# The output projection leaves PSUM through ScalarE, tile 0 shares a bank with tile 2, and GpSimd computes deviation and centre

## What is computed

```python
xn = layernorm(x)                       # mean and variance of each token, eps 1e-5
q, k, v = split(xn @ Wqkv.T + bqkv)     # 16 heads of 16 channels
q, k = rope(q), rope(k)
att = softmax(mask(q @ k.T / sqrt(16))) # causal, 512 x 512 for each head
s = (att @ v) @ Wo.T + bo
g = silu(xn @ sum(factors) / sqrt(8) + bias)
return x + s * g
```

## Time and profile before

| | us |
|---|---|
| median of 3 runs (237.33 to 238.42) | 238.38 |
| the profiled execution, its own time | 237.23 |
| its span | 235.4 |
| PE busy | 219.1 |
| DVE busy | 170.1 |
| ACT busy | 137.7 |
| POOL busy | 109.1 |

### The profile page before, as it was taken

One profiled execution on the slowest core, in us unless ns is written; L12 is line 12 of the kernel. 1 busy time (PEld: TensorE's weight loads), 2 busy tenths in 40 slices (PEclk: granted clock), 3 DMA queues, 4 the chain that ended last, 5 costly groups with the idle time before them and its releaser, 6 DMA issues.

```text
span 235.4 us, 5723 instructions
## 1 busy us (share of the span) xinstructions
PE 219.1 (93%) x2257; PEld 146.3 (62%) x2257; DVE 170.1 (72%) x262; ACT 137.7 (58%) x268; POOL 109.1 (46%) x91
## 2 busy tenths in 40 slices
PE   6999989889979989999989999999999999899992
PEld 2478857566656555656856566658766565585562
DVE  7677999926799875776988859768975796932223
ACT  2422561457932296698525996785168558868940
POOL 7885397362930080192282800672590007029912
PEclk9999999979985899999999999999999999999999
DMA  6996504201510043034009400026034200002002
GB/s 193 348 357 169 161 25 161 89 3 63 172 37 6 3 144 126 8 105 165 4 7 247 158 3 6 3 87 219 11 111 161 93 10 0 4 6 92 0 3 89
DMA packets 15790, 21.47 MB, mean 91 GB/s; under 512 B 2068, under 2 KB 9236, under 8 KB 15764
## 3 DMA queue, kind: packets, MB, share of 16 engines
q1 hardware_dynamic: 15248, 20.06, 26.4%
q0 software_dynamic: 192, 0.52, 0.9%
q10 hardware_dynamic: 324, 0.52, 0.7%
HBM read 6.16 MB, written 2.10 MB: 35 GB/s over the span
## 4 chain that ended last, share of the span: by engine, by line
PE 74%; DVE 17%; issue 4%; ACT 3%; POOL 0%; DVEq 0%; POOLq 0%
PE ring_ps L484 16%; PE ring_ps L521 10%; DVE rowmax L835 9%; PE ring_ps L550 9%; PE ring_ps L607 8%; PE ring_ps L626 7%; PE ring_ps L502 5%; PE ring_ps L494 5%; PE ring_ps L570 3%; PE ring_ps L617 3%; PE ring_ps L676 2%; PE ring_ps L642 2%; ACT probs L942 2%; PE ring_ps L681 2%; DVE y L855 1%
## 5 line engine op out<-in xcount | busy, mean ns | idle before, releaser
L835 DVE TENSOR_REDUCE rowmax<-ring_ps 128x2 f32<-128x1024 f32 (+3 forms) x86 | 86.7, 1046 | 19.4 <-PE ring_ps L502 18.8
L942 ACT ACTIVATE probs<-ring_ps 128x512 f32<-128x512 f32 x160 | 83.7, 611 | 26.5 <-PE ring_ps L502 19.7
L521 PE MATMUL ring_ps<-stack_k,stack_q 62*128 62x512 f32 (+3 forms) x256 | 42.5, 384 | 4.8 <-DVE rowmax L835 4.1
L502 PE MATMUL ring_ps<-ident_bf,masks 64*128 64x64 bf16 (+1 forms) x704 | 39.8, 210 | 0.0
L550 PE MATMUL ring_ps<-stack_q,stack_k 64*128 64x128 f32 (+3 forms) x256 | 37.4, 361 | 1.8 <-DVE rowmax L835 1.8
L484 PE MATMUL ring_ps<-probs,vaug 128*17 128x256 f32 (+3 forms) x528 | 37.8, 426 | 0.7 <-ACT probs L942 0.7
L521 PEld LDWEIGHTS ring_ps<-stack_k,stack_q 62*128 62x128 f32 x256 | 22.9, 193 | 16.3 <-issue 8.9
L502 PEld LDWEIGHTS ring_ps<-ident_bf,masks 64*128 64x128 bf16 x704 | 20.1, 98 | 12.5 <-issue 6.7
L484 PEld LDWEIGHTS ring_ps<-probs,vaug 128*17 128x17 f32 x528 | 13.8, 97 | 21.5 <-issue 16.5
L709 POOL TENSOR_TENSOR parts<-parts,by_sin 128x512 f32<-128x512 f32 x7 | 9.0, 1281 | 39.4 <-DVE by_sin L812 39.4
L550 PEld LDWEIGHTS ring_ps<-stack_q,stack_k 64*128 64x128 f32 x256 | 21.6, 191 | 8.9 <-issue 5.3
(11 more groups left out here) (94 smaller groups left out, 283.1 us busy)
## 6 DMA issues: line engine op xcount, KB each, us to landing
stack_q<-parts SPq DMA_DIRECT2D x48, 128.0 KB, 2.6
stack_k<-parts SPq DMA_DIRECT2D x42, 128.0 KB, 2.6
probs<-factors SPq DMA_DIRECT2D x2, 1024.0 KB, 8.9
out<-result SPq DMA_DIRECT2D x8, 256.0 KB, 2.5
xbuf<-x SPq DMA_DIRECT2D x3, 512.0 KB, 8.2
xbuf<-x SPq DMA_DIRECT2D x2, 256.0 KB, 2.7
probs<-wqk SPq DMA_DIRECT2D x2, 256.0 KB, 5.1
stack_k<-parts POOLq DMA_DIRECT2D x4, 128.0 KB, 3.6
```

Source lines behind the costliest of these rows:

```text
L502: return pe.matmul(diagonal[:, :, half * ROWS:(half + 1) * ROWS], masks[rows, of_maxima, half, :], own, start=False, stop=(half == 1))
L521: pe.matmul(ps[:, s * width:(s + 1) * width], qk[b % 2][0][rows, h // SIDES, tile * P:(tile + 1) * P], qk[b % 2][1][rows, h // SIDES, 0:wi ...
L835: dve.tensor_reduce(of_both, keys, AX_X, ALU.max).then_inc(taken[kind], 2)
L942: act.activation(probs[:, chunk % PROB_SLOTS, :], ps[:, :], ACT.Exp, scale=float(HD) ** -0.5).then_inc(taken[kind], 1)
```

## The change

The output projection's copy out of PSUM moves from DVE to ACT in batches 0 to 2, as a plain copy. The bias now enters as in batch 3 for every batch: GpSimd multiplies gate by bias and adds it to x in the `gate` step, two more instructions of 128x1024 for batches 0 to 2.

A head's tile 0 product goes to the last 128 columns of the bank that holds its tile 2 product. A group has 10 chunks in 5 pairs. PE issues as many products as before. The four masks of such a pair reach over two blocks of 64 columns each (tile 2's and tile 0's), and the four masks of the tile 0 pair are gone: 64 mask matmuls fewer in all. DVE takes such a pair with two reductions, one for each tile: 7 for a group where there were 6.

Deviation and centre are four GpSimd instructions of 128x4. DVE's two are gone. GpSimd also makes the low part of the output weight. The times of all steps and the list of joined pairs are new (18 maxima pairs and 23 scores pairs where there were 20 and 22).

```diff
-MAX_CHUNKS = 12
+MAX_CHUNKS = 10
...
     if c < 8:
-        return 2, [h + c - 4]
-    return (1 if c < 10 else 0), [h + c % 2, h + 2 + c % 2]
+        return [(2, [h + c - 4], 0), (0, [h + c - 4], 3 * P)]
+    return [(1, [h + c % 2, h + 2 + c % 2], 0)]
...
-             ("gate_tanh", 0, 1.217), ("stack", 2, 1.225), ("gate", 0, 1.304), ("shift", 0, 1.329), ("stack", 3, 1.677),
+     ("gate_tanh", 0, 1.232), ("shift", 0, 1.353), ("gate", 0, 1.431), ("stack", 3, 1.518), ("shift", 1, 1.896),
...
             for half in range(SIDES):
-                for ps, tile, heads in both:
-                    width = (tile + 1) * P
-                    keys = ps[:, 0:count_heads * width].rearrange("p (h k) -> p h k", k=width)
-                    mm = masked(pe, keys[:, :, tile * P:], 1, side(heads[0]), half)
+                for ps, parts_of in both:
+                    tile, heads, col = parts_of[0]
+                    last = (len(heads) * (tile + 1) if len(parts_of) == 1 else QT) - 1
+                    diagonal = ps[:, :].rearrange("p (n k) -> p n k", k=P)[:, tile:last + 1:max(last - tile, 1), :]
+                    mm = masked(pe, diagonal, 1, side(heads[0]), half)
...
-                    after(last)
-                    if b > 0:
-                        dve.wait_ge(s_xn, normalised(b - 1))
-                    dve.tensor_scalar(rstd[:], moments[:, :, 1], EPS, None, ALU.add).then_inc(s_moments, 1)
-                elif kind == "centre":
-                    dve.wait_ge(s_pow, count("rstd", b))
-                    dve.scalar_tensor_tensor(out=centre[:], in0=moments[:, :, 0], scalar=-1.0, in1=rstd[:],
-                                             op0=ALU.mult, op1=ALU.mult).then_inc(s_rstd, 1)
+                    last.then_inc(s_moments, 1)
...
+                elif kind == "project_o" and b < B - 1:
+                    act.wait_ge(done_pe[kind], count(kind, b, i))
+                    if b > 0:
+                        act.wait_ge(s_out[i], 16 * b)
+                    act.activation(result[:, i], ps[:, :].rearrange("p (t c) -> p t c", c=C), ACT.Copy
+                                   ).then_inc(taken[kind], 1)
...
-                    pool.tensor_tensor(rstd[:], rstd[:], minus_half[:], ALU.pow).then_inc(s_pow, 1)
...
+                    after(pool.tensor_scalar(rstd[:], moments[:, :, 1], 1.0, EPS, ALU.mult, ALU.add))
+                    after(pool.tensor_tensor(rstd[:], rstd[:], minus_half[:], ALU.pow))
+                    after(pool.tensor_tensor(centre[:], moments[:, :, 0], rstd[:], ALU.mult))
+                    pool.tensor_scalar(centre[:], centre[:], -1.0, 0.0, ALU.mult, ALU.add).then_inc(s_rstd, 1)
...
-                    silu = pool.tensor_tensor(gate[:, b % 2], gate[:, b % 2], gate_t[:], ALU.mult)
-                    if b == B - 1:
...
-                    silu.then_inc(s_gate, 1)
+                    after(pool.tensor_tensor(gate[:, b % 2], gate[:, b % 2], gate_t[:], ALU.mult))
+                    bias_o = bias_sb[:, 2 * C:].unsqueeze(1).broadcast_to([P, QT, C])
+                    after(pool.tensor_tensor(gate_t[:], gate[:, b % 2], bias_o, ALU.mult))
+                    x_b = xbuf[:, b % X_SLOTS]
+                    pool.tensor_tensor(x_b, x_b, gate_t[:], ALU.add).then_inc(s_gate, 1)
```

More of the change, by code:

```diff
@@ new lines @@
+    (("stats", 0, -6.753), ("rstd", 0, -3.783), ("normalise", 0, -1.479), ("turn_x", 0, 0.740), ("turn_x", 1, 0.776),
+     ("project_vg", 0, 1.044), ("project_qk", 0, 1.089), ("project_qk", 1, 1.193), ("project_vg", 1, 1.225),
+     ("project_vg", 2, 1.299), ("rotate", 0, 1.358), ("project_qk", 2, 1.522), ("project_qk", 3, 1.543),
+     ("high", 0, 1.554), ("rotate", 1, 1.598), ("low", 0, 1.694), ("stack", 0, 1.705), ("project_vg", 3, 1.712),
+     ("bias_vg", 0, 1.759), ("stack", 1, 1.867), ("gate_tanh", 0, 1.952), ("high", 1, 2.031), ("stack", 2, 2.043),
+     ("low", 1, 2.173), ("shift", 0, 2.223), ("gate", 0, 2.292), ("stack", 3, 2.320), ("shift", 1, 3.016),
+     ("turn_y", 0, 4.363), ("turn_y", 1, 4.820), ("project_o", 0, 5.177), ("project_o", 1, 5.617),
+     ("store", 0, 12.675), ("store", 1, 13.830)),
@@ new lines @@
+    (("stats", 0, -1.348), ("rstd", 0, 0.743), ("normalise", 0, 1.650), ("turn_x", 0, 1.764), ("turn_x", 1, 1.774),
+     ("project_qk", 0, 1.960), ("project_qk", 1, 1.985), ("project_qk", 2, 2.227), ("rotate", 0, 2.228),
+     ("high", 0, 2.305), ("project_qk", 3, 2.315), ("stack", 0, 2.437), ("low", 0, 2.531), ("stack", 1, 2.635),
+     ("rotate", 1, 3.021), ("project_vg", 0, 3.042), ("high", 1, 3.097), ("project_vg", 1, 3.223),
+     ("project_vg", 2, 3.520), ("project_vg", 3, 3.563), ("low", 1, 3.580), ("bias_vg", 0, 3.581),
+     ("shift", 0, 4.264), ("stack", 2, 4.352), ("gate_tanh", 0, 4.364), ("gate", 0, 4.716), ("stack", 3, 4.751),
+     ("shift", 1, 5.306), ("turn_y", 0, 7.016), ("turn_y", 1, 7.279), ("project_o", 0, 7.661),
+     ("project_o", 1, 7.690), ("store", 0, 16.049), ("store", 1, 22.818)),
@@ L689, in _ @@
                     if b == 0 and i == 0:
-                        pe.wait_ge(s_split, count("split", 0, 3))
+                        pe.wait_ge(s_last_split, 1)
                     if b < B - 1:
```

196 lines of the change are left out of this document (92 added, 104 removed).

## The result

The changed kernel takes 225.69 us (median of 4 executions, 225.26 to 225.78). The kernel before took 237.99 us in the same session (4 executions, 237.33 to 238.42). The ratio is 0.950, with a 95% interval of 0.947 to 0.953. The gain is 12.3 us. The prediction was 232.9 with a range from 227.0 to 238.8, so the direction was right and the size was not. The profiled execution took 225.73 us, its span is 223.9.

A forecast was written before the change was run, and what follows sets the result against it. PE was taken as the bound, with DVE behind it. The terms -2.0 - 4.0 + 0 + 0.5 + 0 = -5.5 us took the profiled 237.2 to 231.7; against the median of 238.4, 232.9 us, range 227.0 to 238.8.

The forecast's parts named there:

- the term of the stretch from 30 to 92 us: Batch 0 and first unit of batch 1: the new order covers waits and DVE has less work, -4.0 us (-9 to 0).
- the row of eight maxima pairs: Ahead of the first values: PE about 0.5 us a pair, DVE over 1 us, so PE waits and the clock falls again.
- rival 1: From 30 to 92 us: the hole closes altogether, second low stretch short; 4 us more gain, 228.9 us, chance 0.14.
- The projection's cover: Ahead of batch 0's shift: a batch 1 projection now stands there and covers the 1.2 us that PE waited.
- DVE's hole behind the shift: From 47.8 us, 9.2 us long: DVE idle 5.8 us, 2.0 us of maxima work put into it.
- DVE's lower load: From 30 to 92 us: DVE loses 1.7 us of work and gains 0.9, so 0.8 us lower.
- The masks: On PE behind 92 us: 0.20 us saved in each of ten groups, -2.0 us (-3.1 to 0).
- The start: Before 30 us: deviation and centre on GpSimd, low part off DVE, 0 us (-0.8 to +1.0).
- The output copies: Moved from DVE to ACT: batch 3's two stand between exponentials, half of 1.0 us on the path, +0.5 us (0 to +1.0).
- The gate: On GpSimd, batches 0 to 2: two more instructions, 14.2 us in all, almost no part of the chain, 0 us.
- Rival 3: Batch 0's longer gate holds up ACT's normalise of batch 2, banks fill, PE idles: +2.5 us, 240.9 us, chance 0.12.
- Rival 2: From 30 to 92 us: the wait only moves, the clock falls as long; 236.9 us (238.4 to 238.9 if masks free), chance 0.18.

The follow-up runs named there:

- the kernel with the cover moved: Changed kernel with project_vg 2 of batch 1 moved from two places ahead of shift 0 of batch 0 to right behind it: 227.36 us, ratio 0.965.
- the order alone: Kernel before (12 chunks) with only the changed kernel's step times and joined pairs: 239.18 us, ratio 1.010.
- the kernel with packing and order alone: Kernel before with tile 0 packed with tile 2 and the new times and joined pairs; other work stays on DVE, gate at two instructions: 226.72 us.
- packing alone: Kernel before with tile 0 products packed into tile 2's bank (ten chunks a group), every step at its old time: 238.88 us, ratio 1.008.
- the two kernels with one step moved: packing alone with turn_x 1 of batch 1 one maxima pair earlier, 237.66 us; the order alone with a batch 2 tile 0 pair behind the next projection, 237.64 us.
- the order with one pair later: the order alone with the tile 0 pair of batch 2's first group moved from ahead of project_vg 1 to behind it: 237.64 us, ratio 1.004.

## Why the prediction was wrong

**The step that failed** is in the term of the stretch from 30 to 92 us: "I do not add the lost clock ... PE will wait there and I expect a low stretch again." The low stretch did not come. The term was -4.0 us and the stretch gave -8.4: the 6.8 us that the prediction had itself worked out from the earlier trace rows came back whole, and PE's idle time fell by 2.2 us where the term had counted 4.0 us of waits and DVE work. That step is 4.4 of the 7.2 us between 232.9 and 225.69. Another 1.4 are the part behind it (-3.4 for -2.0), 0.35 the copies and the end, less 0.2 at the start. The last 1.2 us are the step from the profiled execution to the median, which the changed kernel doesn't have (225.73 and 225.69). The prediction's sum with the 6.8 us added would be -12.3, the number measured between the medians. That would have been luck: it gives the stretch -10.8 for the -8.4 measured.

The reason given was the row of eight maxima pairs at 0.5 us on PE and over 1 us on DVE. That row was read from an excerpt; in PE's queue three projections, two transposes and several scores stand between these pairs, and the timeline shows PE's longest wait there at 0.50 us. Its rival 1, "the hole closes altogether", with a short second low stretch, had the mechanism and nearly the size: -8.0 for the stretch. It got a chance of 0.14. The range ended at 227.0, though the paragraph on the stretch had bounded its gain at 11 us. That the clock stayed up because the waits are short is likely, but not proven: it also stayed up behind the wait of 1.79 us in the kernel with the cover moved, and behind those of 1.69 and 1.24 us with the order alone.

**The parts of that term.** The projection's cover was put at 1.2 us; moving it away cost 1.1 us of span. DVE's hole behind the shift closed: from 47.8 to 57.0 us it is busy 7.43 us where it was 3.44. DVE's lower load, put at 0.8 us, wasn't measured by itself; all the moved work is worth about 1.0 us together. I had named the stretch's end the first `values` of batch 1, and that is not where 92 us lies: it is near the third `values` of batch 0, which came at 90.52 and now comes at 82.28.

**The masks.** L502 is down to 640 and the new pair takes 0.54 us (158.80 to 159.34), both as forecast. Behind 90.52 us PE's busy time fell by 1.8 us for a term of -2.0. The size was right, its name was not: more masks cost nothing, so it must be the four products' own pair with its start and end that is saved. What the term left out is that PE's idle time would fall as well (3.2 to 1.65 us). Ten groups use twenty banks fewer, which may be why. It also left out that the same packing in the old order opens a hole. PE is busy 110.77 of 112.42 us there, 98.5%, where 97% was expected.

**The start** was put at 0 and is +0.2. GpSimd's 4% of the chain after the change lie here, between 20.6 and 30.5 us, with the output weight's low part (1.30 us) and `rstd` (1.05 us) among them. **The output copies**, +0.5 (0 to +1.0), cost nothing: with DVE 225.54, with ACT 225.69. From 195.35 to 214.40 us ACT is busy 16.36 of 19.05 us (15.6 of 19.0), PE 17.96, and the end is 0.15 us longer. **The gate** was put at 0, and nothing speaks against it. GpSimd is busy 18 us more, the gate has no part in the chain, and the kernel with packing and order alone, which lacks the two instructions, is not faster (226.72); it has other work back on DVE too, so the gate isn't priced by itself. The Trainium skill's page "GPSIMD Engine Reference", section "4.1 Engine selection", which has two-input elementwise work on VectorE, would have given 243.0 us by the prediction's working. Its factor of about 2 agrees with this case: in the kernel before, a two-input instruction of 128x512 takes GpSimd 1.29 us (L1059) and DVE 0.68 us. But no run here shows the loss; GpSimd is idle for 43% of the span.

**Rival 3**, the gate that holds up ACT's normalise, was close in its timing. The gate's last instruction on GpSimd and ACT's normalise:

```profile
50.80 2.40 POOL L1058 TENSOR_TENSOR xbuf<-xbuf,xn 128x1024 f32<-128x1024 f32 x1
```

```profile
55.09 2.10 ACT L893 ACTIVATE xn<-xbuf,centre,rstd 128x256 f32<-128x256 f32 x4
```

The gate ended at 53.2, as worked out (53.0). ACT came at 55.09 and not at 53, so there were 1.9 us to spare. **Rival 2**, the wait that only moves, fell in the changed kernel. With packing alone it is what happened: PE's wait of 1.05 us ahead of the tile 0 pair became one of 1.85 us ahead of the projection. In the two kernels with one step moved, the next long wait (1.79 us ahead of shift 0, 1.69 us ahead of shift 1 of batch 2) had been there all along.

**What stays open.** Why the clock falls behind one hole and not behind another (1.19 us and 1.79 us), or behind the same hole in one execution and not in another, isn't settled. How much of the interaction is the ring of 8 banks and how much is DVE's queue wasn't separated beyond the two places shown; a 12-chunk kernel with an order of its own as well fitted as the new one wasn't tried.

## What to carry to other kernels

Where a program fixes the order of its work by hand and shares few buffers, a change of structure and the order fitted to it are one change: cost them together, by the holes that the pair of them leaves on the busiest engine. Shortening a step that covers a wait can gain nothing in itself and only open the wait, as packing did in the old order. When the profile's row of the clock shows low slices and a change closes the holes ahead of them, the slow work (share of lost clock times length) belongs into the sum or at least into the range, as a rival with its own price.

## What the runs showed of the hardware

PE's clock fell from 2.4 to 1.2 GHz behind single holes of 1.2 to 1.9 us. The kernel before in pieces of 4 us from 44 us on:

```profile
44.00:48.00 4.00, 2.24 (x31) 1.40 (x30) 3.72 (x5) 2.68 (x5) 3.21 (x2) 0.99 0.01 4
48.00:52.00 4.00, 4.00 (x29) 2.76 (x28) 0.68 (x1) 1.25 (x3) 2.65 (x3) 0.59 0.01 3
52.00:56.00 4.00, 4.00 (x22) 2.89 (x23) 1.76 (x4) 3.94 (x8) 0.00 (x0) 1.00 0.01 3
```

And the changed kernel with the cover moved, with less work in the first piece and no fall behind it:

```profile
44.00:48.00 4.00, 1.83 (x25) 1.32 (x26) 3.57 (x6) 2.43 (x5) 3.78 (x3) 1.00 0.00 0
48.00:52.00 4.00, 4.00 (x34) 2.99 (x33) 1.66 (x2) 1.80 (x5) 3.92 (x2) 1.00 0.03 8
```

The two kernels differ in much else. A closer pair is the order alone and the order with one pair later: up to batch 2 they have the same instructions in the same order. Both wait 1.69 us at the first shift. With the order alone no fall came behind it:

```profile
38.84 0.60 PE L595 MATMUL ring_ps<-ident,rowmax 128*4 128x128 f32 x4 [1.69 <-DVE rowmax L788]
38.00:46.00 8.00, 6.78 (x62) 4.55 (x62) 6.50 (x10) 2.19 (x4) 3.90 (x4) 1.00 0.06 19
```

With the one pair later it did:

```profile
39.50 0.60 PE L596 MATMUL ring_ps<-ident,rowmax 128*4 128x128 f32 x4 [1.69 <-DVE rowmax L789]
38.00:46.00 8.00, 6.50 (x42) 4.17 (x43) 5.46 (x9) 1.16 (x4) 2.55 (x3) 0.79 0.07 25
```

So the same hole can bring the clock down in one execution and not in another, and the time of a kernel with such holes varies with it (234.7 to 238.9 us for the kernel before, 225.3 to 225.8 for the changed one).

The second thing is that 128 additional bf16 mask matmuls of 64 columns, in place of as many columns in fewer instructions, took 0.2 us of busy time and nothing of the kernel's time.
